# Filter copies shared with VectorE, absolute values moved to ScalarE, and x added with the bias, in a sampled-convolution and state-space hybrid on Trainium2

## The reference, cut to what matters

```python
x = x + deform_conv(_gn(x), offset_w, offset_b, weight, bias)   # x is (8, 32, 16, 16)
#   offsets = conv2d(gn, offset_w) + offset_b                   # 18 channels: dy, dx of 9 taps
#   sampled = bilinear_sample(gn, ys, xs)                       # 9 taps x 8 x 256 places x 32 channels
#   out     = einsum('bkhwc,ock->bohw', sampled, w) + bias
t = _to_tokens(x)                                               # (8, 256, 32)
t = t + state_space(_ln_t(t), ...)                              # 64 state rows, a scan over 256 tokens
t = t + routed_ffn_attention(_ln_t(t), ...)                     # steps chosen by argmax of token 0
x = _from_tokens(t, x)
```

## Time and profile before

| | value |
|---|---|
| median of 3 runs | 319.74 us |
| lowest and highest run | 319.07 and 322.37 us |
| profiled execution: its own time | 321.11 us |
| its span (first to last instruction) | 319.3 us |
| mean granted clock of TensorE, share of full speed | 0.862 |
| convolution up to the sum's last product, in the span | 80.4 us |

### The profile page before, as it was taken

One profiled execution on the slowest core, in us unless ns is written; L12 is line 12 of the kernel. 1 busy time (PEld: TensorE's weight loads), 2 busy tenths in 40 slices (PEclk: granted clock), 3 DMA queues, 4 the chain that ended last, 5 costly groups with the idle time before them and its releaser, 6 DMA issues.

```text
span 319.3 us, 5999 instructions
## 1 busy us (share of the span) xinstructions
PE 255.2 (80%) x2422; PEld 150.1 (47%) x2422; DVE 239.5 (75%) x183; ACT 215.2 (67%) x298; POOL 170.7 (53%) x105
## 2 busy tenths in 40 slices
PE   8698999999796253676697759975898998797983
PEld 3345777776452000243483437543766844233730
DVE  0349999990459999999999999999999943114461
ACT  1047777776277999999999999999975321332351
POOL 1340000000185999999999999999989920000000
PEclk9999999999999755599758795779559789989998
DMA  6200000000013000000000000000000000000001
GB/s 188 108 0 2 2 0 2 2 2 2 0 25 76 0 0 1 0 2 2 1 2 0 2 2 0 2 2 1 1 2 4 0 2 0 12 16 4 0 0 33
DMA packets 2505, 4.00 MB, mean 13 GB/s; under 512 B 687, under 2 KB 1712, under 8 KB 2480
## 3 DMA queue, kind: packets, MB, share of 16 engines
q1 hardware_dynamic: 2216, 3.45, 3.6%
q10 hardware_dynamic: 264, 0.20, 0.2%
HBM read 2.59 MB, written 0.26 MB: 9 GB/s over the span
## 4 chain that ended last, share of the span: by engine, by line
PE 41%; DVE 19%; POOL 18%; issue 11%; DMA 4%; ACT 3%; SPq 1%; DVEq 0%; ACTq 0%; POOLq 0%
POOL pool L445 18%; DVE pool L774 11%; PE ps L981 10%; PE ps L991 5%; PE ps L1118 3%; PE ps L915 3%; PE ps L1107 2%; DMA pool<-x_dram 2%; PE ps L1312 2%; PE ps L1085 2%; PE ps L1029 2%; PE ps L1126 2%; DVE pool L274 1%; PE ps L1063 1%; DMA pool<-w_attn_dram 1%
## 5 line engine op out<-in xcount | busy, mean ns | idle before, releaser
L774 DVE TENSOR_TENSOR_SCAN pool<-ps,pool 128x1024 f32<-128x1024 f32 x63 | 143.9, 2289 | 3.7 <-POOL pool L445 1.2
L445 POOL TENSOR_TENSOR pool<-pool 128x1024 f32<-128x1024 f32 x58 | 134.9, 2350 | 5.6 <-ACT pool L562 4.5
L1085 PE MATMUL ps<-pool,picks 96*128 96x512 bf16 x120 | 49.3, 504 | 40.7 <-DVE pool L774 40.7
L572 ACT ACTIVATE ps<-ps,a_cols 128x1020 f32<-128x1020 f32 x64 | 69.4, 1085 | 8.0 <-DVE pool L751 6.1
L562 ACT ACTIVATE pool<-ps 128x1024 f32<-128x1024 f32 x58 | 59.2, 1020 | 5.4 <-PE ps L1085 2.9
L509 ACT ACTIVATE pool<-ps 128x1024 f32<-128x1024 f32 x36 | 34.9, 1022 | 13.2 <-PE ps L981 13.2
L274 DVE TENSOR_TENSOR pool<-pool 128x2048 f32<-128x2048 f32 x18 | 40.1, 2284 | 0.9 <-ACT pool L490 0.9
L1107 PE MATMUL ps<-pool 128*32 128x112 f32 x1024 | 40.3, 297 | 0.0
L1107 PEld LDWEIGHTS ps<-pool 128*32 128x32 f32 x1024 | 31.4, 126 | 18.0 <-issue 18.0
L408 POOL MEMSET pool<- 128x4096 f32 x1 | 3.5, 3511 | 67.1 <-DVE tn L713 67.1
L1085 PEld LDWEIGHTS ps<-pool,picks 96*128 96x128 bf16 x120 | 7.9, 108 | 61.0 <-DVE pool L774 59.3
(11 more groups left out here) (166 smaller groups left out, 240.4 us busy)
## 6 DMA issues: line engine op xcount, KB each, us to landing
pool<-ssm_w_dram SPq DMA_DIRECT2D x1, 896.0 KB, 9.5
pool<-pool SPq DMA_DIRECT2D x12, 64.0 KB, 2.0
pool<-offset_w_dram SPq DMA_DIRECT2D x1, 576.0 KB, 7.3
cst<-const_dram SPq DMA_DIRECT2D x1, 426.0 KB, 7.9
pool<-x_dram SPq DMA_DIRECT2D x2, 128.0 KB
pool<-conv_w_dram SPq DMA_DIRECT2D x1, 144.0 KB, 7.8
pool<-w_up_dram SPq DMA_DIRECT2D x2, 64.5 KB
out_dram<-pool SPq DMA_DIRECT2D x1, 128.0 KB
```

The costliest lines, as they stand in the source:

```text
L445: pool_e.tensor_tensor(dbx[e % 3], bx, delta_wide[n % 2], ALU.mult).then_inc(pool_dbx_ready, 1)
L572: act.activation(decay[:, :, 1:HW], decay[:, :, 1:HW], ACT.Exp, scale=a_cols[:, PER * g + j:PER * g + j + 1]).then_inc(da_ready, 1)
L774: dve.tensor_tensor_scan(state[e % RING], slot(e), dbx[e % 3], 0.0, ALU.mult, ALU.add)\
L1085: ins = pe.matmul(slot(e)[:, column_half(c)], picks[:, j * 128:(j + 1) * 128], stack[0:96, g * SEQ + c * BANK:g * SEQ + (c + 1) * BANK], s ...
```

## The change

The diff makes five edits.

1. VectorE takes two of the eight filter copies, the second pairs of n = 0 and n = 1 (`take_filters`, counted on `z_taken`); ScalarE keeps six, and its order becomes (0,0), (1,0), (2,0), the first hats, (2,1), (3,0), (3,1).
2. VectorE makes the absolute value for the first iteration alone; from the second on ScalarE makes it (`ACT.Abs`) ahead of its Relu, and now waits there on `hat_diff`. VectorE's distances for the next iteration stand behind chunk j = 1. ScalarE's hats for all later iterations stand behind its copies of chunk j = 0.
3. The product of x with the identity and the closing product of zeros are gone. The first tap_sum opens bank 0 and the last closes it. VectorE waits on `chunk_summed` and adds bias and x in one instruction.
4. `turn_out_rows` and ScalarE's copy of its result stand in the first layer norm, the former where one `keep_warm(4)` was, and use bank 3.
5. `filters(2)` and `filters(3)` have `keep_warm(2)` ahead of each.

```diff
+        def evacuated_by_dve(n, two):
+            return n < 2 and two == 1
+        def evacuated_upto(n, two):
+            return n + 1 if two == 0 and n < 3 else n + two + 2
+        def filter_halves(n, two):
+            half, side = divmod(n, 2)
+            return zs[:, half, 2 * two:2 * two + 2, side, :], \
+                bank(3 + 2 * two, 2).rearrange("p (q k) -> p q k", q=2)[:, :, 0:TAPS * C]
...
             def hats(i):
 
+                act.wait_ge(hat_diff, i + 1)
+                v = hat[:, i, :, :, :].rearrange("p c o y -> p (c o y)")
+                act.activation(v, v, ACT.Abs).then_inc(hat_abs, 1)
                 act.wait_ge(hat_abs, i + 1)
-                v = hat[:, i, :, :, :].rearrange("p c o y -> p (c o y)")
                 act.activation(v, v, ACT.Relu, bias=1.0, scale=-1.0).then_inc(hat_ready, 1)
 
-            evacuate_filters(0)
-            evacuate_filters(1)
-            hats(0)
-            evacuate_filters(2)
-            evacuate_filters(3)
-            act.wait_ge(rows_done, 1)
-            act.activation(out_rows[:, :], bank(0)[:, 0:(BATCHES + 1) * C], ACT.Copy).then_inc(rows_ready, 1)
-            hats(1)
+            evacuate_filters(0, 0)
+            evacuate_filters(1, 0)
+            evacuate_filters(2, 0)
+            act.wait_ge(hat_abs, 1)
+            first_hats = hat[:, 0, :, :, :].rearrange("p c o y -> p (c o y)")
+            act.activation(first_hats, first_hats, ACT.Relu, bias=1.0, scale=-1.0).then_inc(hat_ready, 1)
+            evacuate_filters(2, 1)
+            evacuate_filters(3, 0)
+            evacuate_filters(3, 1)
...
-                    if j == 0 and 0 < it < HALVES * ROWS - 1:
+                    if j == 0 and it < HALVES * ROWS - 1:
                         hats(it + 1)
...
+            act.wait_ge(rows_done, 1)
+            act.activation(out_rows[:, :], bank(3)[:, 0:(BATCHES + 1) * C], ACT.Copy).then_inc(rows_ready, 1)
             act.wait_ge(xs_done, 1)
...
+            def take_filters(n):
+                to, of = filter_halves(n, 1)
+                dve.wait_ge(z_done, 2 * n + 2)
+                dve.tensor_copy(to, of).then_inc(z_taken, 1)
+
+            take_filters(0)
             dve.wait_ge(offT_done, 1)
             distances(0)
+            dve.wait_ge(hat_diff, 1)
+            flat = hat[:, 0, :, :, :].rearrange("p c o y -> p (c o y)")
+            dve.scalar_tensor_tensor(flat, flat, -1.0, flat, ALU.mult, ALU.max).then_inc(hat_abs, 1)
+            take_filters(1)
             for it in range(HALVES * ROWS):
                 for j in range(3):
                     sampling_chunk(dve, it, j)
-                    if j == 0 and it + 1 < HALVES * ROWS:
+                    if j == 1 and it + 1 < HALVES * ROWS:
                         distances(it + 1)
 
-            dve.wait_ge(conv_done, 1)
-            dve.tensor_scalar(t1[:, :], bank(0), part["conv_b"], None, ALU.add).then_inc(ln_in, 1)
+            dve.wait_ge(chunk_summed, 3 * HALVES * ROWS)
+            dve.scalar_tensor_tensor(t1[:, :], bank(0), part["conv_b"], xq, ALU.add, ALU.add).then_inc(ln_in, 1)
...
-                    if n == 2 and q == 0:
-                        turn_out_rows()
-                    if n > 2 and q == 0:
-                        keep_warm(4)
+                    if n > 1 and q == 0:
+                        keep_warm(2)
                     if n and q % 2 == 0:
 
-                        pe.wait_ge(z_ready, 2 * n - 1 + q // 2)
+                        if evacuated_by_dve(n - 1, q // 2):
+                            pe.wait_ge(z_taken, n)
+                        else:
+                            pe.wait_ge(z_ready, evacuated_upto(n - 1, q // 2))
...
-            pe.wait_ge(z_ready, 8)
+            pe.wait_ge(z_ready, 6)
+            pe.wait_ge(z_taken, 2)
...
-                if n == 0:
-                    pe.wait_ge(x_in, 16 * HALVES)
-                    pe.wait_ge(rows_ready, 1)
-                    pe.matmul(bank(0), ident, xq[:, :], start=True, stop=False)
...
-            pe.matmul(bank(0), zero_bf[:, 0:128], zero_bf[:, :], start=False, stop=True).then_inc(conv_done, 1)
...
-                keep_warm(4)
+                if n == 0:
+                    turn_out_rows()
+                else:
+                    keep_warm(4)
```

More of the change, by code:

```diff
@@ L220, in hybrid_kernel @@
             sem, ["off_done", "off_ready", "offT_done", "hat_diff", "hat_ready"])
-        z_done, z_ready = map(sem, ["z_done", "z_ready"])
+        z_done, z_ready, z_taken = map(sem, ["z_done", "z_ready", "z_taken"])
         samp_made = [sem(f"samp_made{j}") for j in range(3)]
-        samp_turned, turned_ready, chunk_summed, conv_done = map(
-            sem, ["samp_turned", "turned_ready", "chunk_summed", "conv_done"])
+        samp_turned, turned_ready, chunk_summed = map(
+            sem, ["samp_turned", "turned_ready", "chunk_summed"])
         ln_in, ln_cen, ln_sq, ln_var, ln_sd, ln_out = map(
@@ L476, in _, with evacuate_filters @@
             act.activation(gsd[:, :], mv[:, :, 1], ACT.Sqrt, bias=eps[:, :]).then_inc(gn_sd, 1)
[L479 to L484, removed]
+            def evacuate_filters(n, two):
+                to, of = filter_halves(n, two)
+                act.wait_ge(z_done, 2 * n + two + 1)
+                act.activation(to, of, ACT.Copy).then_inc(z_ready, 1)
             def hats(i):
+                act.wait_ge(hat_diff, i + 1)
+                v = hat[:, i, :, :, :].rearrange("p c o y -> p (c o y)")
+                act.activation(v, v, ACT.Abs).then_inc(hat_abs, 1)
                 act.wait_ge(hat_abs, i + 1)
-                v = hat[:, i, :, :, :].rearrange("p c o y -> p (c o y)")
                 act.activation(v, v, ACT.Relu, bias=1.0, scale=-1.0).then_inc(hat_ready, 1)
-            evacuate_filters(0)
-            evacuate_filters(1)
-            hats(0)
-            evacuate_filters(2)
-            evacuate_filters(3)
-            act.wait_ge(rows_done, 1)
-            act.activation(out_rows[:, :], bank(0)[:, 0:(BATCHES + 1) * C], ACT.Copy).then_inc(rows_ready, 1)
-            hats(1)
+            evacuate_filters(0, 0)
[7 more added lines that the diff above has]
+            evacuate_filters(3, 1)
             for it in range(HALVES * ROWS):
@@ L684, in distances @@
                                   ALU.subtract).then_inc(hat_diff, 1)
-                dve.wait_ge(hat_diff, i + 1)
-                flat = v.rearrange("p c o y -> p (c o y)")
-                dve.scalar_tensor_tensor(flat, flat, -1.0, flat, ALU.mult, ALU.max).then_inc(hat_abs, 1)
+            def take_filters(n):
[3 more added lines that the diff above has]
+            take_filters(0)
             dve.wait_ge(offT_done, 1)
             distances(0)
+            dve.wait_ge(hat_diff, 1)
+            flat = hat[:, 0, :, :, :].rearrange("p c o y -> p (c o y)")
+            dve.scalar_tensor_tensor(flat, flat, -1.0, flat, ALU.mult, ALU.max).then_inc(hat_abs, 1)
+            take_filters(1)
             for it in range(HALVES * ROWS):
@@ L939, in turn_out_rows @@
                 for b in range(BATCHES + 1):
-                    ins = pe.matmul(bank(0)[:, b * C:(b + 1) * C],
+                    ins = pe.matmul(bank(3)[:, b * C:(b + 1) * C],
                                     by_row[:, b * 128:(b + 1) * 128], wt["w_out"][:, 0:C], start=True, stop=True)
@@ L992, in tap_sum @@
                                         zs[:, half, q, hh, k * C:(k + 1) * C],
-                                        sampT[j][:, q, hh, :], start=False, stop=False)
+                                        sampT[j][:, q, hh, :], start=it + j + hh == 0,
+                                        stop=it == HALVES * ROWS - 1 and j == 2 and hh == 1)
                 ins.then_inc(chunk_summed, 1)
```

## The result

The changed kernel takes 320.69 us in the median of 20 runs (318.37 to 322.71), the kernel before 319.06 us in the median of 20 (317.25 to 322.37). The ratio is 1.0052 with a 95% interval from 1.0029 to 1.0075: **slower by 0.5%**, 0.9 to 2.4 us, where 0.95 us less was forecast.

The account below looks back on a forecast made before the run. TensorE bounds the convolution loop, so only its waits at head and tail count: 0.63 plus 0.32 is 0.95 us gained, from the median 319.74 to 318.8 us; range 317.1 to 321.3 us.

Parts of the forecast that it names:

- the clock rival: Head, 20 to 27 us: thinner TensorE work drops its clock to half, making the kernel slower; chance 0.13.
- the fifth count: Second pair of filters(3) waits for z_ready 5, copy (3,0), starting at 25.42 us instead of about 24.63.
- the short kind: Short low-clock stretch in the loop: costs 1 to 2 us, ending at 320.3 us; half the clock case's 0.13.
- The head's arithmetic: Filters to second turn: step-by-step times put the second turn at 28.82 instead of 29.45 us, 0.63 us gained.
- the later first product: Head: VectorE's product 1 starts at 23.86 us instead of 23.04, 0.82 us later, behind ScalarE's delayed Relu.
- the second product behind it: Head: VectorE's product 2 starts 2.23 us behind the first, at 26.09 us, and ends at 28.38 us.
- the late filters: Head: TensorE's last filter products delay the first turn to 26.92 us instead of 26.18.
- The second turn 1.90 us behind the first: Loop's head: without the product of x (1.02 us), the second turn starts at 28.82 us instead of 29.45.
- ScalarE's slack: Loop: ScalarE's copies end at 33.4 us, TensorE wants them at 33.62; slack of 0.2 us, thin but enough.
- The tail: Loop's end: VectorE's bias addition starts 0.04 us behind the last sum, at 80.14 instead of 80.46; 0.32 us gained.
- The layer norm's cost of 0: First layer norm: row products end at 85.22 us, transposes start at 85.25; cost 0 to 0.15 us, taken as 0.
- the long kind: Low-clock stretch of 13 us in the loop: costs 6.5 us, ending at 325.3 us; half the clock case's 0.13.

Follow-up runs that it names:

- edit 1 alone: Kernel before with only the VectorE filter copies, ScalarE's new copy order and their waits: ratio 1.0065, head and loop 64.20 us.
- the fourth count: Changed kernel, second pair of filters(3) waiting for copy (2,1) instead of (3,0), no zero products added: ratios 0.9979 and 1.0013.
- the gaps filled: Changed kernel plus zero products: three ahead of the second pairs of filters(2) and filters(3), four ahead of the first turn: ratio 1.0006.
- edit 3 alone: Kernel before without the product of x and closing product, VectorE adding bias and x: ratio 0.9970, head and loop 61.62 us.
- edit 1 undone: Changed kernel with ScalarE making all eight filter copies in the old order, edits 2 to 5 kept: ratios 0.9940 and 1.0002.
- the rows behind the norm: Changed kernel without edit 1, the layer norm's four zero products back and row products behind its transposes: ratio 0.9957.
- two of five edits: Kernel before with edits 2 and 3, filter copies, row products and zero products as they were: ratios 0.9923 and 0.9943.

## Why the prediction was wrong

**The step that failed** is the one that set the clock rival's chance: "before, the clock stayed at 1.00 through the same filters and through the wait", and "as many zero products remain". Neither carries over. The prediction named the new waits, and held that the old products would carry the clock over them. In the trace two new waits of TensorE (0.52 us for VectorE's copy, 0.75 us for the fifth count) stand between the filter pairs, close ahead of the old one in front of the first turn (0.75, before 0.92 us). With these waits the clock falls even where all the old products are kept: edit 1 alone has the row products, all four zero products and the product of x, and fell; its trace shows only the wait for the fifth count as a new gap. The clock fell in three profiles of three, where I gave 0.13. The mechanism and the price of the short kind were right: "costs 1 to 2 us and ends at 320.3 us"; the median is 320.69, and the three heads lost 0.75, 1.96 and 0.72 us against before, 1.7 to 2.9 us against the forecast.

**The head's arithmetic was right to 0.15 us** for the later first product, the second product behind it and the late filters. That the fifth count instead of the fourth costs 0.8 us at the first turn was also right (0.85 measured). What I didn't see is that the same wait decides the clock: with the fourth count it stayed at 1.00 twice. I had also put the least difference that can be told at about 1%; the intervals came out at 0.2 to 0.4% to either side, narrow enough to show the loss.

**The second turn 1.90 us behind the first** holds only at full clock: 3.66 us for both with the gaps filled, 5.38 without.

**ScalarE's slack** held. VectorE does wait for the hats in the loop, 5.6 us in five waits in the changed kernel, but TensorE doesn't wait for VectorE because of it:

```profile
DVE pool L274 <- ACT pool L504: 5.6, 5, 1.4
```

In the changed kernel the slow turns gave ScalarE more time than the forecast had. It held at full clock as well: with the gaps filled TensorE waits for ScalarE once in the loop, ahead of the last sum, as the kernel before does.

```profile
78.37 1.07 PE L1019 MATMUL ps<-pool 128*32 128x256 f32 x16 [0.21 <-ACT pool L524]
```

**The tail** was 0.32 us by the working. From the start of the last sum to that of the bias addition it is 1.14 us in the changed kernel and with edit 3 alone, 1.43 before: 0.29 us gained. The stretch of edit 3 alone is only 0.23 us shorter, since its second turn starts 0.07 us later.

**The layer norm's cost of 0** was right in all three profiles of the changed kernel. Over all programs with edit 4's layer norm, three profiles of nine show a fall there of 1.4 to 1.7 us; of the nine with zeros in that place, none does. That edit 4 brings these falls is likely by this count, and not shown. One pair of kernels ran side by side and differs in this stretch alone (edit 1 undone, the second time, and the rows behind the norm); there the kernel with zeros is 1.3 us lower in the median, 317.47 against 318.77, though its profiled head fell. But in its first group the other one had the ratio 0.9940, no worse than 0.9957. Its share in the loss of the changed kernel stays open; the heads alone, 1.1 us in the mean of three, lie inside the interval of 0.9 to 2.4 us.

**The transposes.** The Trainium skill, "TensorE: Matmul & The Clock Gate", Part 4, has it that transposes don't count as busy as other products do. By that, I had said, the long kind of fall would be the likely one. The runs say otherwise: in the first profile the clock came back after 3.4 us while TensorE ran 32 transposes and nothing else, in the second after some 7 us in the same turns, and the loop of two thirds transposes kept it at 1.00 to its end.

## What to carry to other kernels

Before work is taken off a busy TensorE, or a wait is put between its products, list what it does in the microseconds ahead of the next stretch that it bounds: products that nobody waits for can hold up the clock of the microseconds that follow, 3 to 7 of them here. Test such a place in both directions, once with filler added and once with filler taken away. Where a copy's order changes, count each semaphore value against the order of the increments; a wait that is one count too long changes no result and may cost twice, as a wait and as the clock. And keep the parts of a change apart: here two of five edits gain 0.6 to 0.8%, and one alone loses 0.65%.

## What the runs showed of the hardware that was not expected

No single wait of TensorE among the filters ahead of the falls at the head was longer than 1.01 us, and it had been at full clock for some 25 us. The length of one wait doesn't decide: the kernel with the fourth count waits 1.12 us ahead of its first turn and keeps its clock, twice. What about the waits decides stays open. The low stretches at the head lasted 3 to 7 us. Between heads that are the same program one cost 1.4 us (61.24 against 59.88 and 59.85 us); the longest made its head 1.2 us longer than the two others of the same kernel. The same instructions fall in one execution and not in the next (the head without edit 1 and without row products once of three, the layer norm without edit 1 once of two, the start of the kernel before once of two), so a single profile doesn't clear a kernel of it. VectorE's copy of 576 columns from PSUM took 0.76 us, ScalarE's 0.65.
